# LoRA rows of eight sequences in three operands of 256 columns instead of four

## The reference

```python
gate = x @ Wg + (x @ Ag[idx]) @ Bg[idx]      # Wg 512 x 2048, rank 16, 8 adapters
up   = x @ Wu + (x @ Au[idx]) @ Bu[idx]
h    = silu(gate) * up
x    = x + h @ Wd + (h @ Ad[idx]) @ Bd[idx]  # Wd 2048 x 512
x    = x + einsum('bct,bcd->bdt', x, W[idx]) # 64 x 64 for each sequence
```

## Time and profile before

| what | value |
|---|---|
| median of 3 runs | 1187.9 us (1187.41 to 1190.95) |
| profiled execution | 1185.85 us |
| span of its instructions | 1184.2 us |
| TensorE matmuls | 1152.3 us busy, 6726 matmuls |
| VectorE | 968.9 us busy |
| ScalarE | 587.8 us busy |
| gather of B rows | 512 DMAs of 64 KB, median 2.2 us from issue to landing |

### The profile page before, as it was taken

The page is one execution under the profiler, slowest core; times in us unless marked ns, Lnnn a source line. Parts: engine busy times, 40 slices in busy tenths (PEclk is TensorE's granted clock), DMA queues, the critical chain, the costliest instruction groups (busy, mean ns, idle before and its releaser), DMA issues.

```text
span 1184.2 us, 22189 instructions
## 1 busy us (share of the span) xinstructions
PE 1152.3 (97%) x6726; PEld 1026.4 (87%) x6726; DVE 968.9 (82%) x1639; ACT 587.8 (50%) x958; POOL 243.1 (21%) x390
## 2 busy tenths in 40 slices
PE   7899999999999999999999999997999999999998
PEld 5788888888888888888888888887999999999997
DVE  6988898988898988889898999986777667767774
ACT  6555454654454645445465455554444444444442
POOL 3133111123211124311111111112323212321220
PEclk9999999999999999999999999999999999999999
DMA  6485455566555468545558676587777777677771
GB/s 212 140 263 175 139 163 157 177 232 174 161 173 155 134 196 297 178 136 166 155 183 278 177 219 201 160 282 250 266 232 246 244 267 241 233 257 263 250 253 58
DMA packets 147496, 241.05 MB, mean 204 GB/s; under 512 B 21458, under 2 KB 90194, under 8 KB 147250
## 3 DMA queue, kind: packets, MB, share of 16 engines
q1 hardware_dynamic: 124912, 180.94, 48.1%
q0 software_dynamic: 21744, 57.57, 15.3%
q10 hardware_dynamic: 722, 1.13, 0.3%
HBM read 169.30 MB, written 70.25 MB: 202 GB/s over the span
## 4 chain that ended last, share of the span: by engine, by line
PE 82%; DVE 7%; DMA 3%; ACT 3%; issue 3%; SPq 1%; DVEq 0%; ACTq 0%
PE ps L1363 16%; PE ps L1364 16%; PE ps L1365 15%; PE ps L1374 9%; PE ps L1531 7%; PE ps L1533 7%; PE ps L1532 7%; DMA h_raw<-h_dram 3%; PE ps L1392 2%; DVE hl L854 1%; ACT xo_hi L561 1%; ACT hh L561 1%; DVE w_lo L854 1%; DVE xst L865 1%; SPq L194 1%
## 5 line engine op out<-in xcount | busy, mean ns | idle before, releaser
L1363 PE MATMUL ps<-xo_hi,w_hi 128*128 128x512 f32 x882 | 350.0, 397 | 3.8 <-ACT u_s L630 3.1
L1364 PE MATMUL ps<-xo_lo,w_hi 128*128 128x512 f32 x882 | 346.1, 392 | 0.0
L1365 PE MATMUL ps<-xo_hi,w_lo 128*128 128x512 f32 x882 | 343.4, 389 | 0.0
L447 POOL DMA_DIRECT2D h_dram<-hs x128 | 96.2, 756 | 542.3 <-DVE hs L992 274.6
L854 DVE TENSOR_TENSOR hl<-h_raw,hh 128x1024 fp32r<-128x1024 f32 x112 | 136.9, 1223 | 82.8 <-ACT hh L561 81.8
L1365 PEld LDWEIGHTS ps<-xo_hi,w_lo 128*128 128x128 f32 x882 | 165.7, 188 | 36.8
L1363 PEld LDWEIGHTS ps<-xo_hi,w_hi 128*128 128x128 f32 x882 | 166.5, 189 | 33.9 <-ACT u_s L630 5.2
L1364 PEld LDWEIGHTS ps<-xo_lo,w_hi 128*128 128x128 f32 x882 | 166.5, 189 | 25.3
L1374 PEld LDWEIGHTS ps<-t_st,bq 128*128 128x128 f32 x1024 | 156.2, 189 | 22.6 <-issue 2.3
L561 ACT ACTIVATE hh<-h_raw 128x1024 fp32r<-128x1024 f32 x112 | 118.0, 1053 | 114.2 <-DMA h_raw<-h_dram 72.5
L1374 PE MATMUL ps<-t_st,bq 128*128 128x256 f32 x1024 | 162.6, 282 | 1.9 <-DVE t_st L854 1.9
(11 more groups left out here) (160 smaller groups left out, 2333.6 us busy)
## 6 DMA issues: line engine op xcount, KB each, us to landing
h_raw<-h_dram SPq DMA_DIRECT2D x112, 512.0 KB, 5.4
bq_raw<-b_twice SPq DMA_DIRECT2D x512, 64.0 KB, 2.2
h_dram<-hs POOLq DMA_DIRECT2D x128, 256.0 KB, 4.2
raw<-packed SPq DMA_DIRECT2D x58, 512.0 KB, 4.6
h_dram<-h_f SPq DMA_DIRECT2D x96, 256.0 KB, 3.1
ad_raw<-a_d SPq DMA_DIRECT2D x64, 128.0 KB, 2.2
xs<-x POOLq DMA_DIRECT2D x16, 512.0 KB, 4.9
y_out_dram<-xs POOLq DMA_DIRECT2D x30, 256.0 KB, 4.7
```

What stands on the lines that cost most here:

```text
L447: pool.dma_start(h_dram[PPG * g:PPG * (g + 1), op, :, k, :].rearrange("q p t -> p q t"), tile[:, col:col + HALF].rearrange("p (q t) -> p q ...
L1363: pe.matmul(bank, st[0], mv[0], start=start and kk == 0, stop=False, skip_group_check=True)
L1364: pe.matmul(bank, st[0], mv[1], start=False, stop=False, skip_group_check=True)
L1365: m = pe.matmul(bank, st[1], mv[0], start=False, stop=kk == 1, skip_group_check=True)
```

## The change

Eight sequences have 8 x 16 x 3 = 384 rows of the three wanted products (high-high, high-low, low-high; low-low is dropped), which are three operands of 128 rows instead of four. The first operand covers columns 0 to 255 of the pair's 512 (its sequences 0 to 3), the middle one columns 128 to 383 (sequences 2 to 5), the third columns 256 to 511 (sequences 4 to 7). The rows of sequences 2 to 5 with the high part of B (high-high, high-low) lie in the middle operand, their rows with the low part of B in rows 0 to 31 of an outer one; all other rows lie in the outer two, those with the low part of B in rows 32 to 63.

- gather fetches 48 rows a sequence: one DMA of 48 rows, or one of 16 and one of 32 for the four sequences of a pair that have rows in the middle operand. A pair takes 12 DMAs where it took 8.
- bq_hi writes a high part of 64 rows and 1024 columns into a buffer of its own (bq_high), bq_lo subtracts it in place; a new ScalarE function bq_rest rounds the other rows in place: the middle operand (128 rows, 512 columns) and rows 64 to 127 of the outer two (1024 columns).
- t_hi becomes three ScalarE copies (64 rows x 512, 32 x 512, 32 rows x 256 columns), t_mask two VectorE operations, t_lo two (512 and 256 columns). t_st is cleared once at the start by four memsets on VectorE.
- order_a and order_a_first copy in two halves, for another order of sequences; a_raw has two buffers.
- new waits: TensorE for bq_rest_done and t_rest_done, bq_hi for bq_lo_done, t_mask for t_rest_done, and a few on constants.

The core of the diff:

```diff
-GATHER = SLOTS // 2 * 16
+PARTS = 3
+GATHER = 12 * 16
             def gather(n, b):
                 g, k = divmod(n, PIECES)
-                sp.dma_start(bq_raw[n % 2][b % QS:P:QS, b // QS, 1, :, :].rearrange("r k c -> r (k c)"),
-                             b_twice[piece_of(g, k), bass.ds(slot_numbers[g * SLOTS + b], 1)].rearrange("a r c -> (a r) c"))\
-                    .then_inc(bq_in[2 * b // SLOTS][n % 2], 16)
+                pair, j = divmod(b, SLOTS // 2)
+                q, two = divmod(j // 2, 2)
+                first = two == (q == 0)
+                own, mid, row = 2 * q, 64 * q + j % 2, j % 2
+                rows = [(own, row, 32, RANK), (1, mid, 64 * q + 64, 2 * RANK)] if first else [(own, 32 + row, P, 3 * RANK)]
+                for part, lo, end, count in rows:
+                    sp.dma_start(bq_raw[n % 2][lo:end:2, pair, part, :, :].rearrange("r k c -> r (k c)"),
+                                 b_thrice[piece_of(g, k), bass.ds(slot_numbers[g * SLOTS + b], 1), 0:count]
+                                 .rearrange("a r c -> (a r) c")).then_inc(bq_in[pair][n % 2], 16)
...
             def order_a(g, q):
...
-                pool.tensor_copy(aq[0][:, :, :, :], a_raw[0][:, :, :, :].rearrange("p s k r -> p k r s")).then_inc(a_ordered, 1)
+                for i in range(2):
+                    two = 2 * (1 - i if q % 2 == 0 else i)
+                    m = pool.tensor_copy(aq[0][:, :, i, :, :],
+                                         a_raw[g % 2][:, two:two + 2, :, :].rearrange("p s k r -> p k r s"))
+                m.then_inc(a_ordered, 1)
...
             def bq_hi(n, pair):
-                q = slice(2 * pair, 2 * pair + 2)
                 act.wait_ge(bq_in[pair][n % 2], GATHER * (n // 2 + 1))
-                if n >= 2:
-                    act.wait_ge(p4_done, 2 * n - 2)
-                hi(bq[n % 2][:, q, 0, :, :], bq_raw[n % 2][:, q, 1, :, :]).then_inc(bq_hi_done, 1)
+                act.wait_ge(bq_lo_done, bq_turn(n, pair))
+                hi(bq_high[0:64, :, :, :], bq_raw[n % 2][0:64, pair, 0:PARTS:2, :, :]).then_inc(bq_hi_done, 1)
+
+            def bq_rest(n, pair):
+                hi(bq[n % 2][:, pair, 1, :, :], bq_raw[n % 2][:, pair, 1, :, :])
+                hi(bq[n % 2][64:P, pair, 0:PARTS:2, :, :], bq_raw[n % 2][64:P, pair, 0:PARTS:2, :, :]).then_inc(bq_rest_done, 1)
...
             def t_hi(g, q):
...
-                hi(t_st[0][g % 2][0:QR, cols], t_f[0:QR, :]).then_inc(t_hi_done, 1)
-                hi(t_st[1][g % 2][QR:P, cols], t_f[QR:P, :]).then_inc(t_hi_done, 1)
+                hi(t[0:64, pair, 2 * h, :, :], t_f[:, :, :]).then_inc(t_hi_done, 1)
+                hi(t[64:96, pair, 2 * h, :, :], t_f[32:64, :, :])
+                hi(t[64 * h:64 * h + 32, pair, 1, :, side], t_f[0:32, :, c]).then_inc(t_rest_done, 1)
...
             bq_hi(0, 0)
+            bq_rest(0, 0)
             order_a_first(2)
...
             bq_hi(0, 1)
+            bq_rest(0, 1)
             t_hi(0, 3)
...
                 if more:
                     w_hi_sum(s + 1, 1)
+                bq_rest((s + 1) // 2, s % 2)
                 if last:
                     x_hi(g + 1, 2)
...
             def lora(bank, s, u, pair, start):
                 g, c = divmod(s, CH)
                 b = bq[(s // PIECE) % 2]
-                for part in range(2):
-                    for i in range(2):
-                        q = pair * 2 + i
-                        m = pe.matmul(bank[:, i * QT:(i + 1) * QT], b[:, q, part, c % PIECE, u * P:(u + 1) * P],
-                                      t_st[u][g % 2][:, q * QT:(q + 1) * QT], start=start and part == i == 0,
-                                      stop=part == i == 1, skip_group_check=True)
+                for i in range(PARTS):
+                    m = pe.matmul(bank[:, i * P:i * P + QT], b[:, pair, i, c % PIECE, u * P:(u + 1) * P],
+                                  t_st[g % 2][:, pair, i, u, :], start=start and i == 0, stop=i == PARTS - 1,
+                                  skip_group_check=True)
                 return m
...
                 if s % PIECE == 0:
                     pe.wait_ge(bq_lo_done, s + 2)
+                    pe.wait_ge(bq_rest_done, s + 2)
                 lora(RB[par], s, 0, 0, False).then_inc(p2_done, 1)
```

More of the change, by code:

```diff
@@ L54, with cond_resid_kernel @@
 KIB4 = 4096
-def cond_resid_kernel(nc, x, xg, idx, packed, wd, a_gu, b_twice, a_d, b_d, w1, slot_mask, tok_mask, eye, out):
+def cond_resid_kernel(nc, x, xg, idx, packed, wd, a_gu, b_thrice, a_d, b_d, w1, slot_mask, tok_mask, eye, out):
     ctx = ExitStack()
@@ L95, in cond_resid_kernel @@
[L95 to L98, removed]
+        bq = [at(f"bq{i}", 147456 + i * 16384, [P, 2, PARTS, PIECE, WB], F32R) for i in range(2)]
+        bq_raw = [at(f"bq_raw{i}", 147456 + i * 16384, [P, 2, PARTS, PIECE, WB]) for i in range(2)]
+        bq_high = at("bq_high", 159744, [P, 2, PIECE, WB], F32R)
+        t_st = [at(f"t_st{i}", 176128 + i * 12288, [P, 2, PARTS, 2, QT], F32R) for i in range(2)]
@@ L932, in t_mask @@
                     dve.wait_ge(t_lo_done, 2 * i)
+                    dve.wait_ge(t_rest_done, i)
                 bank = T_BANKS[q] if g == 0 else RT
-                dve.tensor_tensor(t_f[:, :].rearrange("p (b t) -> p b t", t=SEQ),
-                                  bank[:, 0:QT].rearrange("p (b t) -> p b t", t=SEQ),
-                                  smask[:, :].unsqueeze(2).to_broadcast([P, QS, SEQ]), ALU.mult).then_inc(t_masked, 1)
+                for u in range(2):
+                    rows = slice(u * QR, (u + 1) * QR)
+                    m = dve.tensor_tensor(t_f[:, u, :].rearrange("p (b t) -> p b t", t=SEQ),
+                                          bank[rows, 0:QT].rearrange("p (b t) -> p b t", t=SEQ),
+                                          smask[rows, q % 2, :].unsqueeze(2).to_broadcast([QR, QS, SEQ]), ALU.mult)
+                m.then_inc(t_masked, 1)
             def t_lo(g, q):
                 i = g * QUADS + q
-                cols = slice(q * QT, (q + 1) * QT)
-                gate, up = t_st[0][g % 2], t_st[1][g % 2]
-                dve.wait_ge(t_hi_done, 2 * i + 1)
-                lo(gate[QR:P, cols], t_f[0:QR, :], gate[0:QR, cols]).then_inc(t_lo_done, 1)
-                dve.wait_ge(t_hi_done, 2 * i + 2)
-                lo(up[0:QR, cols], t_f[QR:P, :], up[QR:P, cols]).then_inc(t_lo_done, 1)
+                pair, h = divmod(q, 2)
+                t, c, side = t_st[g % 2], slice((1 - h) * P, (2 - h) * P), slice(h * P, (h + 1) * P)
+                dve.wait_ge(t_hi_done, i + 1)
+                lo(t[96:P, pair, 2 * h, :, :], t_f[32:64, :, :], t[32:64, pair, 2 * h, :, :]).then_inc(t_lo_done, 1)
+                lo(t[64 * h + 32:64 * h + 64, pair, 1, :, side], t_f[0:32, :, c], t[0:32, pair, 2 * h, :, c])\
+                    .then_inc(t_lo_done, 1)
             def make_c11(s):
@@ L1168, in x_first @@
                 x_lo(0, XOPS.index(op))
+            for i in range(2):
+                for pair in range(2):
+                    m = dve.memset(t_st[i][:, pair, 1, :, :].bitcast(F32), 0.0)
+            m.then_inc(t_zeroed, 1)
             x_first(B11)
```

90 lines of the change are left out of this document (57 added, 33 removed).

## The result

The changed kernel takes 1194.75 us (median of 17 runs), the kernel before 1188.52 us on the same chip: ratio 1.0049 (95% interval 1.0036 to 1.0061, as for every ratio below). It is slower by 0.5%, where 1177.9 us and "faster" were predicted, and lies above the range of 1165 to 1189 us that was to hold it eight times in ten. The profiled execution has a span of 1193.5 us against 1184.2.

The account below looks back on a forecast made before the run. The prediction took the TensorE to bound the gate/up stage: 30.1 - 6.7 - 8.7 - 3.7 - 1.0 = 10.0 us gained, from a median of 1187.9 to 1177.9 us; eight-in-ten range 1165 to 1189 us.

Parts of the forecast that it names:

- 256 matmuls: TensorE, gate/up stage: each lora() issues three matmuls for four, 256 fewer at 0.1175 us, saving 30.1 us.
- stall of even steps: TensorE's lora waits for ScalarE's bq_rest in 28 even steps, 0.24 us each: 6.7 us lost, bounds 0 and 10.
- changes of group: Steps 15/16, 31/32, 47/48: little VectorE room and bq_rest ahead of x_hi(2) cost 2.9 us three times, 8.7 us.
- startup: Added bq_rest and longer t_hi on ScalarE delay the start; with the first steps' lost saving 3.7 us, bounds 1 and 6.
- end of the stage: Last three steps: VectorE and ScalarE, also splitting wd, give back 1.0 us, bounds 0 and 2.
- SyncE: Eight more gather issues a turn, 5.2 us, fit into SyncE's 7 us wait: 0 us lost, bounds 0 and 8.
- rival three: SyncE's issuing of the gathers becomes the bound of the stage, 51 us more: 1229 us; chance 0.10.
- One: Rival: ScalarE's tail is covered in even steps, a change of group costs at most 1 us: 1166 us; chance 0.15.
- Two: Rival: VectorE binds all steps with 11.12 us, stalls reach their upper bounds: 1186.5 us, no change; chance 0.15.

Follow-up runs that it names:

- x by PoolE: The changed kernel with load_x moved from SyncE's program into PoolE's, at the same step: 1186.17 us, ratio 0.9987.
- x spread: The changed kernel with load_x still on SyncE, its four 512 KB transfers spread over three steps: 1186.62 us, ratio 0.9987.
- all three rearrangements: x by PoolE with queues reordered in even steps (bq_rest ahead of second w_hi_sum), last steps of groups and startup: 1175.44 us, ratio 0.9893.

## Why the prediction failed, point by point

| term | predicted, us | measured in the trace, us |
|---|---|---|
| 256 matmuls | +30.1 | +30.1 (11.52 to 11.04 a step) |
| stall of even steps | -6.7 (28 x 0.24) | -11.5 (28 x 0.41) |
| changes of group | -8.7 | -9.7 |
| startup | -3.7 | -5.6 |
| end of the stage | -1.0 | -1.0 |
| SyncE | 0, bounds 0 and 8 | -10.9 |

**SyncE is the step that failed.** The prediction took a turn of the queue from the mean wait of 7 us and from four batches of gathers away from load_x, put all else in a turn at 5.0 us, and left out that once a group four loads of x stand in it. It looked at the mean room and asked whether it is enough; the question was in which turn the room is least. The account of SyncE's order ahead of the prediction leaves load_x out as well. In the trace of before that turn had 5.6 us of room and not 7, and eight more gathers took 7.7 us there and not 5.2. So in that turn rival three's mechanism happened, at three places for 10.9 us (beyond the bound of 8) and not everywhere for 51. The second half of the error was the price of being late. That "pair 0 is wanted over a step later" left the landing out: the gather of that turn took 9.0 us to land before and 9.07 after, so before the change it had half a microsecond to spare, and behind its bq_hi stands keep_u2. x by PoolE and x spread both take this loss away. This loss alone made the kernel slower than the one before: without it, 1186.2 us against 1187.5. It does not account for the whole miss. Of the 18.6 us between the forecast gain of 10.0 and the loss of 8.6 that the terms of the table make, SyncE is 10.9, the even steps 4.8, startup 1.9 and the changes of group 1.0.

By the Trainium skill (DMA: Bandwidth & Descriptors, Rules for kernel authors) small DMAs pay mostly overhead below 64 KB, which spoke for rival three. The trace agrees as far as landing goes (32 KB in 2.4 us, 96 KB in 2.9), and the same bytes in twelve DMAs cost 1192.63 us for 1187.46. The Trainium skill says in the same section that another engine's queue saves only issue time. Spreading x on SyncE's own queue gave as much as PoolE's (both 0.9987), so no run here speaks against it.

**The even steps: right mechanism, undersized.** The prediction put bq_rest's start 1.02 us behind keep_u2's, and 249.99 - 248.97 is that. The two copies took 1.69 us for 1.58, and the TensorE started 0.14 us behind their end, where 0.06 was taken from a wait for keep_u2. The lateness is thus 0.33 us for 0.14, and the slower first matmuls 0.08 for 0.10. A margin of 0.14 us can't be had from a sum of rows in which two terms are off by 0.11 and 0.08 us; its upper bound, 0.35, was exceeded as well by the 0.41.

**The changes of group: the size right, the place partly.** bq_rest ahead of x_hi(2) did what was said: the idle time ahead of x_lo went from 0.21 to 1.93 us. Rearranging the queue gives back 1.5 us each. The 2.4 us at c = 9 come from the VectorE's work in the step ahead, which the prediction named (step 8 of a group). Step 48 keeps 12.3 us in every order tried, but steps 47 and 48 have to be read together: 23.81 us before, 25.31 after, 24.26 with the matmuls alone left out and 24.56 with all three rearrangements. So most of what is left there was lost without any addition of the change; what ends the last 0.3 us was not tried.

**Startup: the chain right, undersized.** lora of step 0 waited 4.11 us for t_st (1.89 before), as said. What it mis-sized is the delay, 4.6 us for 2.9: t_hi of quad 3 started 4.3 us later than before (35.40 for 31.13) where 2.2 had been worked out. The prediction saw the eight more gathers, and that pair 1 lands "about when ScalarE's later queue asks for it"; in the kernel after its last gather landed at 31.0 and bq_hi started at 32.75 without a wait. Mending the order was worth 0.7 us only, since the added ScalarE work stays ahead of keep_u2 in the order tried. Twelve gathers alone cost 2.1 us in steps 1 and 2 of the kernel before, where bq_hi did wait for them (1.49 us); how much of that is in the 5.6 was not separated.

**The rivals.** One (tail covered) fell: lora waits for bq in 25 steps. Two (VectorE binds all steps) fell for the ordinary step, which has 11.04 us where 11.12 of loop had been read: that loop was read in step 13, where a half x_add of 0.68 us stands in it (at 188.33 in the trace of before), and steps without one have more room. But the VectorE decides what mended versions can reach: some 6 us of the 30 with the matmuls alone, and 4.1 of the even steps' 11.5.

## What to carry to other kernels

A queue that has room in the mean is not free: find the turn in which everything that it issues falls together, and add the new work there. A step that is inserted into an in-order queue costs what stands behind it, so a place is chosen by which of the later ones is least urgent: the same 1.69 us cost 0.41 in an ordinary even step in one place, 0.20 in another and nothing in a third. A transfer's room has to be counted from its issue to the moment its data is read, landing included, and in the turn where both are worst. And taking time off the engine that bounds a stage pays until the next loop's own length (here some 6 of 30 us were lost to that with nothing added).

## What the runs showed of the hardware

The granted clock of the TensorE behind the stall in step 36 of the kernel after (window, its length, busy time of each engine, granted clock, DMA share, GB/s):

```profile
459.30:465.40 6.10, 6.08 (x29) 4.71 (x27) 3.67 (x7) 1.33 (x2) 1.63 (x3) 1.00 1.06 371
465.40:471.30 5.90, 0.17 (x1) 0.00 (x0) 1.47 (x2) 2.56 (x5) 0.00 (x0) 0.74 0.84 204
471.30:474.90 3.60, 3.57 (x10) 2.99 (x11) 2.85 (x5) 2.08 (x3) 1.52 (x2) 0.50 1.00 289
```

After 5.76 us without work the clock stood at 0.50, the lower of the two levels (1.2 GHz), for the next 3.6 us: product matmuls came 0.43 us apart in place of 0.23. Six product matmuls and three of lora took 3.37 us there (471.33 to 474.70) where six of 0.23 and 0.35 make 1.73, so by this estimate the long stall cost some 1.6 us beyond its length. Behind a short one, as at 251.82 above, the next products keep 0.23.

A gather's DMA instruction took 0.520 us on SyncE in the median and 0.472 before; the two batches of twelve shown above took 7.96 and 10.07 us, 0.66 and 0.84 each. With twelve gathers alone the median was 0.496. Why it is longer (three sizes of rows, other destinations, more traffic) was not tried.
